# A selective-scan stage: which states take a diagonal, and where a copy and a gate stand in the queues

## What is computed

```
dA_t,i,s = exp(delta_t,i * A_i,s)
h_t,i,s  = dA_t,i,s * h_(t-1),i,s + (delta_t,i * u_t,i) * B_t,s
y_t,i    = sum over s of h_t,i,s * C_t,s  +  u_t,i * D_i
out_t    = (y_t * silu(z_t)) @ out_proj_w.T
```

## Time and profile before

| | us |
|---|---|
| median of 3 runs (1178.46 to 1181.62) | 1178.94 |
| the profiled execution, its own time | 1179.91 |
| its span in the trace | 1178.0 |
| its scan stage, first scan to first product after the last | 123.8 to 482.8 |

### The profile page before, as it was taken

How to read it: one execution, slowest core, us unless ns; L and a number is a source line. 1 busy time by engine, 2 the same in 40 slices (tenths; PEclk the granted TensorE clock), 3 DMA queues, 4 the chain that set the end, 5 groups by cost and what they waited for, 6 DMA issues and landing times. The chain is left out here.

```text
span 1178.0 us, 23589 instructions
## 1 busy us (share of the span) xinstructions
PE 1069.0 (91%) x7860; PEld 793.2 (67%) x7860; DVE 889.8 (76%) x1939; ACT 831.1 (71%) x1728; POOL 516.2 (44%) x321
## 2 busy tenths in 40 slices
PE   3877799999999999989969999999999999996997
PEld 3433688988988998779945454545455554546897
DVE  7797988988888889657627686868686867674565
ACT  4997988898898898546626575757575757571565
POOL 0389898898998998434510001010101001011354
PEclk9997799999999999999989999999999999998999
DMA  3001364555785785243320000000000000002331
GB/s 96 4 3 40 83 159 129 144 157 140 207 247 140 196 232 139 68 118 100 107 60 19 1 1 19 2 19 1 19 1 19 8 12 15 6 19 60 102 99 50
DMA packets 107670, 89.50 MB, mean 76 GB/s; under 512 B 35703, under 2 KB 85628, under 8 KB 107552
## 3 DMA queue, kind: packets, MB, share of 16 engines
q1 hardware_dynamic: 98672, 66.01, 21.9%
q0 software_dynamic: 5568, 12.66, 3.0%
q10 hardware_dynamic: 3312, 9.33, 2.6%
HBM read 71.49 MB, written 17.39 MB: 75 GB/s over the span
## 5 line engine op out<-in xcount | busy, mean ns | idle before, releaser
L1084 DVE TENSOR_TENSOR_SCAN h<-d_a,p_dbu 128x1024 f32<-128x1024 f32 x128 | 289.7, 2279 | 30.9 <-ACT d_a L828 25.4
L770 POOL TENSOR_TENSOR h<-h,c_rep 128x1024 f32<-128x1024 f32 x126 | 297.7, 2392 | 22.4 <-DVE h L1084 21.6
L1412 POOL DMA_INDIRECT expert_rows<-r_row,r_dest x60 | 59.1, 985 | 470.0 <-DVEq L1307 455.4
L2060 ACT ACTIVATE arena<-arena,at_min 128x512 f32<-128x512 f32 x256 | 182.3, 720 | 96.6 <-DVE at_min L2170 90.2
L2170 DVE CUSTOM_DVE_ANT_0 arena<-at_p_scores,arena 128x512 f32<-128x512 f32 x256 | 174.1, 684 | 59.5 <-PE at_p_scores L1928 56.7
L828 ACT ACTIVATE d_a<-arena,a_exp 128x511 f32<-128x511 f32 x256 | 168.0, 710 | 13.9 <-DVE h L1084 13.8
L1935 PEld LDWEIGHTS at_p_probs_T<-ident,arena 128*128 128x128 f32 x1024 | 111.9, 141 | 93.2 <-issue 64.9
L1928 PE MATMUL at_p_scores<-arena,at_q_T 64*128 64x512 f32 x512 | 159.3, 641 | 1.5 <-DVE arena L2158 1.5
L1935 PE MATMUL at_p_probs_T<-ident,arena 128*128 128x128 f32 x1024 | 157.3, 281 | 3.2 <-ACT arena L2060 1.8
L976 PE MATMUL p_y_T<-ident,h 128*128 128x128 f32 x1024 | 132.5, 273 | 1.2 <-DVE h L1139 1.1
L820 ACT ACTIVATE b_du_T<-arena,b_T 128x256 f32<-128x256 f32 x304 | 128.7, 495 | 0.0
(11 more groups left out here) (264 smaller groups left out, 1606.7 us busy)
## 6 DMA issues: line engine op xcount, KB each, us to landing
c_rep<-c_rows SPq DMA_DIRECT2D x128, 256.0 KB
diag_b<-diag_rows SPq DMA_DIRECT2D x52, 256.0 KB, 4.2
f_row<-expert_rows SPq DMA_DIRECT2D x78, 129.0 KB
arena<-in_w_all ACTq DMA_DIRECT2D x8, 578.0 KB
arena<-bias_by_distance ACTq DMA_DIRECT2D x8, 448.0 KB
x_tok<-in_x SPq DMA_DIRECT2D x4, 512.0 KB, 6.0
x_tok<-x_between SPq DMA_DIRECT2D x8, 256.0 KB, 2.8
diag_rows<-diag_b SPq DMA_DIRECT2D x4, 256.0 KB, 3.0
```

Of the source, the lines that this page charges most:

```text
L770: nc.gpsimd.tensor_tensor(h_at(n), h_at(n), cc, ALU.mult).then_inc(prod_done, 1)
L1084: nc.vector.tensor_tensor_scan(h_at(n).rearrange("p c t -> p (c t)"), da[:, s % 2, :, :].rearrange("p c t -> p (c t)"), p_dbu[:, s % 2, :, ...
L2060: nc.scalar.activation(pr[:, slot, :], sc[:, slot, :], ACT.Exp, scale=-1.0, bias=mn[:, slot:slot + 1]).then_inc(probs_ready, 1)
```

## The change

`DIAG` names states 8, 10 and 12 in place of 9, 11 and 13; the number of diagonal states in a full turn stays 7, and in the first turn it goes from 3 (11, 13, 15) to 2 (12, 15). `take_g(0)` goes from before the exponentials of state 6 to behind them. `act_normed` goes from behind the exponentials of state 11 to behind those of 12. The `gate` goes from behind scan 2 to behind scan 3.

```diff
-    DIAG = (1, 3, 6, 9, 11, 13, 15)
+    DIAG = (1, 3, 6, 8, 10, 12, 15)
...
             def early(b, s, after_scale):
 
-                if s in (6, 7) and after_scale:
-                    take_g(b, s - 6)
+                if s == 7 and after_scale:
+                    take_g(b, 1)
                 elif s == 10 and after_scale:
                     rt.act_rstd(act, b)
...
-                    if number > 0 and s == 11:
+                    if number > 0 and s == 6:
+                        take_g(b - 1, 0)
+                    if number > 0 and s == 12:
                         rt.act_normed(act, b - 1)
...
             def early(b, s):
-                if s == 2:
+                if s == 3:
                     gate(b)
...
-            early(B - 1, 2)
+            early(B - 1, 3)
```

## The result

The changed kernel takes 1197.8 us (median of 4 runs, 1194.82 to 1198.85) against 1178.7 for the kernel before on the same chip (1178.34 to 1181.62): a ratio of 1.0149, with an interval of 1.0126 to 1.0172. It is slower by 19 us; 1196.3 was forecast.

What follows compares the result with a forecast made beforehand. No engine has much slack, so queue order decides each wait in the scan stage. Turn 0 at 0, turn 1 at 2.2, turns 2 to 6 at 12.35 and turn 7 at 2.8 sum to 17.35: 1196.3 us, range 1187 to 1202.

Steps and rivals of the forecast that it cites:

- The gate's chain: PE's queue behind the gate: gate 1.69 us later, scan 5 waits 1.6, scan 7 comes 1.45 late per turn.
- The diagonal of 8 behind `project`: On PE, a diagonal spread of state 8 costs another 0.8 us, making scan 8 2.27 late.
- my split of the 2.47: Per-turn cost: 1.45 by the gate, 0.8 by the diagonal of 8, 0.2 by scalings of 13 and 14 on ACT.
- this walk: Slots followed through the queues, on ACT from scan 8: next turn at 260.55 instead of 258.08, 2.47 us more.
- nothing gained beyond the walk above: Moving the normed rows behind the exponentials of 12 on ACT was worth nothing more.
- Scans 13 and 14: They take over waits that go at scans 12 and 15, then wait some 1.1 us each for ACT.
- the rstd steps and `take_du`: On ACT, before the exponentials of 10, they were taken to hold it for 1.38 us.
- with the same waits: Turns 3 to 7 of the kernel before were taken as 44.95 us each, with turn 2's waits.
- The clock: Rival (c): PE's clock falls after 2.3 us idle, costing 3.6 more per turn; 42.6 in all, 1221 us; chance 0.03.
- Turn 0: ACT's extra work there costs 0, bound 0 to 0.8 us, as DVE's 8-column copy seems to end with POOL's product.
- scan 5 is not at 226.3: Rival (b), faster: PE catches up, the spread of 5 is there at 226.3, 6.0 us gained, 1173 us; chance 0.06.
- the diagonals were not free: Rival (a): gate's chain costs as forecast but the diagonal part is free; 10.2 us, 1189 us; chance 0.10.

Runs made afterwards that it cites:

- the gate alone: Kernel before with only the gate moved behind scan 3: 1198.07 us, ratio 1.012.
- the diagonals alone: Kernel before with only the new list of diagonal states: 1188.17 us, ratio 1.0036.
- the best kernel here: Kernel before with take_g(0) behind the exponentials of 6, take_du(0) behind those of 9 and act_normed behind those of 12: 1166.58 us, ratio 0.9898.
- old-list run: Changed kernel with DIAG as before, all else as changed: 1191.93 us, ratio 1.0103.
- the copy alone: Kernel before with only take_g(0) moved behind the exponentials of state 6: 1179.84 us, ratio 1.0011.
- the gate back: Changed kernel with the gate behind scan 2 again: 1186.68 us, ratio 1.003.
- the maximum: Kernel before with moved take_g(0), take_du(0) and act_normed, and DVE's 8-column copy written as a maximum of the row with itself: 1166.81 us, ratio 0.9901.
- the normed rows alone: Kernel before with only act_normed moved behind the exponentials of state 12: 1173.71 us, ratio 0.9945.

## Why the prediction was right

**The gate's chain: right, in place and size.** The forecast was that scan 5 would wait 1.6 for PE; it waits 1.60, and moving the spread of 5 ahead of `through_d` takes that wait away from scan 5 and 0.9 us out of the turn. Scan 7 was to be 1.45 late and is 1.50 (234.17 against 232.67). By the runs the gate costs 1.52 per turn alone and 1.25 within the change.

**The diagonal of 8 behind `project`: right in place**, scan 8 is 2.20 late against 2.27 forecast. But my split of the 2.47 into 1.45, 0.8 and 0.2 holds for this walk only. The runs show that the parts don't add: at full clock the gate alone costs 1.52, the diagonals alone 0.80, the copy -0.23 and the normed rows -1.02, in sum 1.07, and together they cost 2.12. What I had wrong is the price of the **normed rows** by themselves. Within the change, "nothing gained beyond the walk above" came out (45.79 without them and the copy, 45.86 with both, in kernels with the gate behind scan 2). But with the old list they gain 1.0 per turn, and the new list takes that gain away. This fits the new list's price of 1.45 when it comes on top of the rest, against 0.80 alone; but 0.80 and 1.02 would make 1.82, and which part gives back the rest no run tells. Scans 13 and 14 wait 1.12 and 1.02 for ACT, as forecast (1.1 each).

**A term mis-sized: the rstd steps and `take_du`.** I took 1.38 from a turn in which they ran in another surrounding; they held ACT for 245.90 - 244.74 = 1.16 in the changed kernel. With that the turn is 2.25 longer, against 2.12 measured. The other turns of the kernel before are not as even as "with the same waits" has it: turns 2 to 6 take 44.97 to 45.50, turn 7 43.92. Turn 2 against turn 2 is not touched by that.

**The clock: the mechanism was right, its share was not.** I gave it a chance of 0.03, as a fall in every turn for 3.6 us. It fell in two turns of seven, and cost 1.6 each: 3.3 us of the 18.4. The wait ahead of `through_d` was 2.14 (2.3 forecast). Only `through_d` and part of the sum behind it ran at 1.2 GHz, not all three slots. The Trainium skill ("TensorE: Matmul & The Clock Gate", Part 1) has the rule that the gate goes by how busy the engine was; the traces agree: with the wait filled with products the clock stayed at 1.00 in seven turns of seven, and with PE idle there it fell in 10 of 18, counted over three kernels.

**The total** came out within 1.5 us of the forecast in part by luck, since two errors cancelled: the turns at full clock are 0.35 shorter than walked, 2.3 us in all, and the clock added 3.3. **Turn 0: right.** DVE reached the 8-column copy later, and the copy got shorter:

```profile
168.75 1.62 DVE L1228 COPY next_row<-first_row 128x8 f32<-128x8 f32 x1
```

so that turn 0 took 45.0 in both kernels. The other rivals fell: scan 5 is not at 226.3, and the diagonals were not free.

## What to carry to other kernels

Where all queues are nearly full, an instruction moved to save a wait of its own engine must be followed into the queue of whoever waits for it: here 0.86 us saved on DVE became a loss of 1.5 a turn, because PE had its next spread behind that wait. The order inside a stretch in which one engine is always busy is worth something if another full engine is fed from it; look for the gap on the second engine (PE's 1.56) before calling it free. Prices of such moves don't add, so price each part again with the others in place, and run the parts one by one: the best kernel here takes two of the four parts and one move that the change doesn't have.

## What the runs showed of the hardware

**PE's clock can fall behind an idle time of 1.6 us, and need not behind one of 2.5.** These are all of PE's waits of over 1.2 us at a clock of 1.00, from state 8 of turn 0 on, in all fourteen traces. A fall is counted where it began in the wait or within 1.8 us of its end:

| PE's wait, us | waits | falls |
|---|---|---|
| 1.22 to 1.39 | 13 | 0 |
| 1.51 to 1.80 | 20 | 2 |
| 2.13 to 2.49 | 18 | 10 |
| 3.27 to 4.85 | 9 | 9 |

The 18 waits are those for the gate in the changed kernel, the gate-alone and the old-list run; behind the ten falls `through_d` took 2.66 to 3.67 in place of 2.05. The two falls behind shorter waits came in kernels without the gate's move, in turn 6 with the copy alone and in turn 4 with the diagonals alone. This is the copy's, with the clock ahead of the wait's end and in the fall:

```profile
426.82 1.55 PE L958 MATMUL p_dbu<-ident,b_du_T 128*128 128x128 f32 x8 [1.71 <-ACT b_du_T L820]
428.21 1.76 PE L978 MATMUL p_y_T<-ident,h 128*128 128x128 f32 x8
429.76 2.91 PE L955 MATMUL p_dbu<-diag_b,arena 128*128 128x128 f32 x16
```

```profile
423.00:426.80 3.80, 2.11 (x20) 1.88 (x19) 3.44 (x2) 3.71 (x9) 3.80 (x3) 1.00 0.62 136
428.40:431.70 3.30, 3.30 (x18) 3.30 (x17) 2.29 (x1) 3.30 (x8) 3.30 (x2) 0.50 0.98 290
```

These two turns were longer by some 1.8 us (46.60 against 44.76) and 2.1 us (47.94 against 45.82, with the gate back). What decides between a fall and none at the same wait, no run here shows. So such waits make a kernel's time vary from run to run as well.

**A tiny DVE instruction can wait for POOL's running product.** In thirteen traces the copy of 8 columns took 1.58 to 4.71 us, and in the fourteenth the maximum took 2.38. Each time it ended 0.02 to 0.03 us behind one of POOL's products of 128x1024: in the run with the diagonals alone, at 171.03, POOL's product at 171.00.

```profile
167.07 3.96 DVE L1226 COPY next_row<-first_row 128x8 f32<-128x8 f32 x1
...
154.64 16.36 POOL L770 TENSOR_TENSOR h<-h,c_rep 128x1024 f32<-128x1024 f32 x7
```

A semaphore is not the cause: in the kernel nothing is waited for ahead of the copy but what the scan before it waited for, and the trace counts the time as the copy's own. The same line of the kernel before, issued again where POOL runs no product, takes 0.17:

```profile
601.08 0.17 DVE L1226 COPY next_row<-first_row 128x8 f32<-128x8 f32 x1 [5.02 <-PEq L159]
```

Whether it gets in at the next end of a product or the one after is worth some 2.3 us, and in the run with the diagonals alone and the one with the normed rows alone turn 0 took 47.4 in place of 45.0. PE then stood idle for 3.27 and 4.03 us, and its clock fell at the start of turn 1. The Trainium skill ("GPSIMD Engine Reference", section 1, Specifications) says that POOL shares its ways into SBUF with DVE, and names DVE's two-port modes and instructions with two SBUF inputs; the maximum has two such inputs and waited just the same, which agrees. The copy has one input, and whether it ran in a two-port mode no run here shows. Why other small steps of the router, such as the reciprocal at L1304 (0.17), do not wait beside running products, no run here settles.
